# The three-valued weights of the second feed-forward layer, prepared one stage earlier

## The chip, the cores and the metric

The kernel runs on one core of one Trainium2 chip. The metric is the device time of one execution in microseconds; the median of three runs is shown. The core has five engines that run at the same time, each with its own queue of instructions that it works through in order: TensorE (PE, matrix products into PSUM; its weight loads are shown apart as PEld), VectorE (DVE), ScalarE (ACT), GpSimd (POOL), and SyncE (SP), which here only issues DMAs. They wait for each other by semaphores: an instruction raises one when it is done, and a wait in another engine's queue holds that queue until the count is reached. PSUM has eight banks of 128 x 512 fp32.

## The reference, cut to what matters

Eight layers run one after the other on x of 1024 rows and 512 columns, each as `x = x + layernorm(layer(layernorm(x)))`. The change touches the second feed-forward layer (L1 ffn), whose weight is made three-valued before it is used, and the attention ahead of it (L1 attention), in whose code it puts work:

```python
x = x + _layernorm(_L1_attn_ref(_layernorm(x), wq, bq, wk, bk, wv, bv))
x = x + _layernorm(_L1_ffn_ref(_layernorm(x), weight))     # weight: 512 out x 512 in

def _L1_ffn_ref(x, weight):
    def binarize_weights(weight):
        scale = mean(abs(weight), axis=1, keepdims=True)
        bin_no_grad = scale * sign(weight)
        clipped = clip(weight, -1.0, 1.0)
        return bin_no_grad - clipped + clipped
    return einsum('bsi,oi->bso', x, binarize_weights(weight))
```

The weights depend on no activation: they could be prepared at any time after their load.

## The kernel before, in words

The program is a row of blocks (`nc.Block()`). In a block every engine has its own code, and no engine begins the next block before all of them have come to the end of this one. Within a block the order of an engine's instructions is the order in which the code is written; there is no scheduler.

Around the change there are three blocks.

1. **The block of the L1 attention** (`small_attn`, name `l1a`, rope true). 32 heads in 8 groups of 4, each in 2 halves of the rows: 16 units of 16 steps, 256 steps in all (`TOTAL`). In a step PE makes two products of scores (L1654), ACT two exponentials of 128x512 (L1784), and PE the products of older exponentials with the values (L1671). DVE reduces the maxima of a later unit: one pair of tiles a step (`reduce_pair`, L1829), 24 steps ahead, so that the last pair stands at step 231. It also scales the finished output of a unit (`finish`, L1839 and L1842) when PE has turned it (`o_turn`, L1686): unit 14 at step 245, unit 15 behind the loop. In the last 16 steps PE adds a product of 128 columns per step that nobody reads (`idle`, L1679). The weight of L1 ffn is loaded by a DMA that SP issues after the first unit's maxima.
2. **The block of the norms** (`renorm`, class `Norms`). Two layer norms over eight tiles of 128 rows: DVE makes the statistics and the sum (L166 to L182), GpSimd the inverse root (L212), ACT the scaled tile `f` (L242), PE turns it with four transposes per tile into PSUM bank t (L282), and ACT copies it to `yT` (L260), the last but one by DVE. PE fills some of its waits with products that nobody reads (L271): six ahead of tile 4, five ahead of tile 6, three behind tile 7.
3. **The block of L1 ffn** (`l1_ffn`). DVE waits for the weight, takes the scale (L494, L496) and then, for each of four tiles `o` of 128 output rows, makes `pos` in six instructions of 128x512 (L500 to L510); a semaphore `s_b` counts them. PE turns each tile of `pos` with four transposes into banks 0 to 3 (L538), ACT copies it to `wT` (L519), and PE waits for all four copies (`pe.wait_ge(s_wT, KC)`). Then PE makes the rows: eight tiles of 128 rows, four products of 128x512 each (L544), 32 in all, which the trace shows as 64 since an fp32 product runs in two passes here. The norms of this layer follow in the same block, tile by tile behind the rows: DVE, GpSimd, ACT and PE by the same class `Norms`. SP's queue in this block issues the four loads of the next attention's weights (`l2a`).

Of the kernel before, what the change touches and what calls it, by code (L numbers as in the profile page):

```python
# [7 lines left out]
P = 128  # L8
T = 1024
NT = T // P  # L10
D = 512
KC = D // P
LN_EPS = 1e-5

ALU = mybir.AluOpType
ACT = mybir.ActivationFunctionType
AX = mybir.AxisListType
F32 = mybir.dt.float32
# [106 lines left out]
class Norms:  # L125
# [111 lines left out]
    def scale(self, act, n, p):  # L237

        chip, nc = self.chip, self.chip.nc
        act.wait_ge(chip.sem("ln_ready"), self.count("ready", (n, p), 1))  # L240
        for t in (2 * p, 2 * p + 1):
            nc.scalar.activation(chip.f[:, t, :], chip.x[:, t, :] if n else self.src(t), ACT.Identity,  # L242
                                 bias=chip.applied[:, n, 1, t:t + 1],
                                 scale=chip.applied[:, n, 0, t:t + 1]).then_inc(chip.sem("ln_scaled"), 1)
# [59 lines left out]
    return Norms(chip, True, chip.last, rows, src, turn_bank, by_halves)  # L304


def renorm(chip, add_f, loads=None):


    if chip.normed:  # L310
        chip.normed = False
        return
    norms = Norms(chip, bool(add_f), False, src=lambda t: chip.f[:, t, :], turn_bank=lambda t: t)
    with chip.nc.Block() as block:
        @block.sync
        def _(sp):
            if loads:
                loads(sp)

        @block.tensor  # L320
        def _(pe):
            norms.tensor(pe)

        @block.vector
        def _(dve):
            for k in range(len(norms.steps)):
                norms.vector(dve, k)
            norms.vector_end(dve)

        @block.gpsimd  # L330
        def _(pool):
            norms.gpsimd(pool)

        @block.scalar
        def _(act):
            norms.scalar(act)


# [120 lines left out]
def l1_ffn_weights(chip, a):  # L459

    w = Weights(chip, "l1f")
    w.w = w.sb("w", [P, KC, D])
    w.transfers(1)

    def loads(sp):
        w.load(sp, w.w[:], weights_view(a["l1f_w"]))
    w.loads = loads
    return w


def l1_ffn(chip, add_f):

    nc, ps, yT = chip.nc, chip.ps, chip.yT
    ahead = chip.take_ahead()
    w = ahead.w
    renorm(chip, add_f)
    s_row, b_row = chip.shared("rows", NT)
    s_b, s_t, s_wT = (chip.sem("l1f_" + n) for n in ("binary", "turned", "wT"))
    with ExitStack() as mem:
        def sb(n, shape, dt=F32):  # L480
            return mem.enter_context(nc.sbuf_tensor("l1f_" + n, shape, dt, side=ahead.side))
        pos, neg, wT = sb("pos", [P, KC, D]), sb("neg", [P, KC, D]), sb("wT", [P, KC, D])
        sc = sb("scale", [P, KC])

        def bank(t):
            return (4 + t) % 8
        following = chip.next_weights()
        norms = stage_norms(chip, (s_row, b_row), lambda t: ps[:, bank(t), :], bank)
        with nc.Block() as block:
            @block.vector  # L490
            def _(dve):
                ahead.wait(dve)
                n = 0
                nc.vector.tensor_reduce(sc[:], w[:], AX.X, ALU.add, apply_absolute_value=True).then_inc(s_b, 1)  # L494
                dve.wait_ge(s_b, 1)
                nc.vector.tensor_scalar(sc[:], sc[:], 1.0 / D, None, ALU.mult).then_inc(s_b, 1)  # L496
                dve.wait_ge(s_b, 2)
                for o in range(KC):
                    k = 2 + 6 * o
                    nc.vector.tensor_scalar(pos[:, o, :], w[:, o, :], 0.0, sc[:, o:o + 1], ALU.is_gt,  # L500
                                            ALU.mult).then_inc(s_b, 1)
                    nc.vector.tensor_scalar(neg[:, o, :], w[:, o, :], 0.0, sc[:, o:o + 1], ALU.is_lt,
                                            ALU.mult).then_inc(s_b, 1)
                    nc.vector.tensor_scalar(w[:, o, :], w[:, o, :], 1.0, -1.0, ALU.min, ALU.max).then_inc(s_b, 1)
                    dve.wait_ge(s_b, k + 3)
                    nc.vector.tensor_tensor(pos[:, o, :], pos[:, o, :], neg[:, o, :], ALU.subtract).then_inc(s_b, 1)
                    dve.wait_ge(s_b, k + 4)
                    nc.vector.tensor_tensor(pos[:, o, :], pos[:, o, :], w[:, o, :], ALU.subtract).then_inc(s_b, 1)
                    dve.wait_ge(s_b, k + 5)
                    nc.vector.tensor_tensor(pos[:, o, :], pos[:, o, :], w[:, o, :], ALU.add).then_inc(s_b, 1)  # L510
                for k in range(len(norms.steps)):
                    norms.vector(dve, k)
                norms.vector_end(dve)

            @block.scalar
            def _(act):
                for o in range(KC):
                    act.wait_ge(s_t, o + 1)
                    nc.scalar.copy(wT[:, :, o * P:(o + 1) * P],  # L519
                                   ps[:, o, :].rearrange("p (c q) -> p c q", c=KC)).then_inc(s_wT, 1)  # L520
                norms.scalar(act)

            @block.gpsimd
            def _(pool):
                norms.gpsimd(pool)

            @block.sync
            def _(sp):
                if following:
                    following.loads(sp)  # L530
                norms.sync(sp)

            @block.tensor
            def _(pe):
                for o in range(KC):
                    pe.wait_ge(s_b, 2 + 6 * (o + 1))
                    for c in range(KC):
                        mm = nc.tensor.transpose(ps[:, o, c * P:(c + 1) * P], pos[:, o, c * P:(c + 1) * P],  # L538
                                                 chip.ident[:])
                    mm.then_inc(s_t, 1)  # L540
                pe.wait_ge(s_wT, KC)
                for t in range(NT):
                    for c in range(KC):
                        mm = nc.tensor.matmul(ps[:, bank(t), :], yT[:, c, t * P:(t + 1) * P], wT[:, c, :],  # L544
                                              start=c == 0, stop=c == KC - 1)
                    mm.then_inc(s_row, 1)
                norms.tensor(pe)
    ahead.mem.close()
# [634 lines left out]
SPAN = T // HALVES  # L1183
# [92 lines left out]
def small_attn(chip, add_f, name, kv_heads, rope):  # L1276
# [3 lines left out]
    nc, ps, f, yT = chip.nc, chip.ps, chip.f, chip.yT  # L1280
# [5 lines left out]
    w = chip.take_ahead()  # L1286
# [3 lines left out]
    with ExitStack() as mem:  # L1290
        def sb(n, shape, dt=F32):
            return mem.enter_context(nc.sbuf_tensor(f"{name}_{n}", shape, dt, side=w.side))
# [3 lines left out]
        q = sb("q", [P, SLOTS, 2, T], F32R)  # L1296
        k = sb("k", [P, SLOTS, KP, T], F32R)
# [5 lines left out]
        mrow = sb("mrow", [4 * QT, P], F32R)  # L1303
        rden = sb("rden", [P, 2, QT, GROUP])
        if rope:
            tmp, res, ab = sb("tmp", [P, 4, SPAN]), sb("res", [P, 2, 2, SPAN]), sb("ab", [P, 2, 2, SPAN])
            s_bias, s_rot, s_pt, s_vb = (chip.sem(f"{name}_{n}") for n in ("biased", "rotated", "pool_rotated", "v_biased"))

        def by_heads(rows):
# [22 lines left out]
        TOTAL = UNITS * STEPS  # L1332
        BEFORE = PAIRS_OF_MAX + AHEAD
        BETWEEN = 18 if rope else BEFORE
        upto = [FIRST_PIECES + -(-(PIECES - FIRST_PIECES) * min(m, BETWEEN) // BETWEEN) for m in range(BEFORE + 1)]
        TAIL = TOTAL - STEPS
        FIRST_TURN = PAIRS_OF_MAX + 1

        s_proj, b_proj = chip.shared("sa_qk", NJ)
# [115 lines left out]
        with nc.Block() as block:  # L1455
# [338 lines left out]
            def _(dve):  # L1794
# [40 lines left out]
                def finish(n):  # L1835
                    g, half = divmod(n, HALVES)
                    dve.wait_ge(s_ot, b_ot + n + 1)
                    both = banks(("out", n))[:, 0, :].rearrange("p (t h e) -> p t h e", h=GROUP, e=2 * HD)
                    nc.vector.reciprocal(rden[:, n % 2], both[:, :, :, HD]).then_inc(s_rd, 1)  # L1839
                    dve.wait_ge(s_rd, b_rd + n + 1)  # L1840
                    rows = f[:, half * QT:(half + 1) * QT, g * GROUP * HD:(g + 1) * GROUP * HD]
                    nc.vector.tensor_tensor(rows.rearrange("p t (h e) -> p t h e", e=HD), both[:, :, :, 0:HD],  # L1842
                                            rden[:, n % 2].unsqueeze(3).broadcast_to([P, QT, GROUP, HD]),
                                            ALU.mult).then_inc(s_out, 1)
# [13 lines left out]
                for at in range(TOTAL):  # L1858
                    for m in max_at.get(at, []):
                        reduce_pair(m)  # L1860
                    n = unit_ended(at, TURN_OUT_STEP)
                    if n is not None:
                        finish(n)
                finish(UNITS - 1)
    if not rope:
        rows_out(chip, name, w)
# [974 lines left out]
```

## Time and profile before

| | |
|---|---|
| median of three runs | 2408.6 us (2408.6, 2408.64, 2401.95) |
| the profiled execution, its own time | 2398.62 us |
| its span in the trace | 2396.8 us |
| granted clock of PE, mean | 0.962 |
| PE busy | 2176.2 us (91%) |
| DVE busy | 1526.9 us (64%) |
| ACT busy | 1307.3 us (55%) |
| GpSimd busy | 643.5 us (27%) |
| the loop's last step to the first work of the norms | about 1413 to 1415.6 us in the trace |
| the block of the norms | 1415.6 to 1439.6 us |
| the block of L1 ffn | 1439.8 to 1499.7 us |

Times inside the trace are microseconds from the start of the span. The profiled execution is one execution, with the hardware profiler on. The busy shares are means over stages that are limited by different things; a change in one stage is read from that stage's rows alone. A row of the timeline gives the start, the duration from first to last instruction of the group, the engine, the line, what is written and read, and in brackets how long the engine had been idle and what ended that. The granted clock (PEclk) is the share of TensorE's full 2.4 GHz; 0.50 is 1.2 GHz.

### The profile page before, as it was taken

The numbers are of one execution on the slowest core, as the hardware profiler recorded it, in microseconds if no ns is written. First come the engines' busy times: TensorE is split into PE (matmuls) and PEld (weight loads), VectorE is DVE, ScalarE is ACT, GpSimd is POOL, SyncE is SP. The second block draws the span as 40 slices with busy tenths as digits, with TensorE's granted clock in tenths as the row PEclk, the third lists the DMA queues.
The fourth block names the chain that finished last, engine by engine and source line by source line (L and its number), as shares of the span: only waits on it lengthen the run. The fifth ranks groups of instructions, "written<-read, shape, count | busy, mean of one in ns | idle before, by whom it ended". The sixth has DMA issues, their size and how long they took to land. (4 is left out here: it accounts for less than half of the span.)

```text
span 2396.8 us, 35809 instructions
## 1 busy us (share of the span) xinstructions
PE 2176.2 (91%) x13122; PEld 1351.4 (56%) x13122; DVE 1526.9 (64%) x2211; ACT 1307.3 (55%) x2192; POOL 643.5 (27%) x529
## 2 busy tenths in 40 slices
PE   6998999999999798999999977799999998999877
PEld 4666777777777585444444444334444445877453
DVE  3575777777777434589999935149999935333253
ACT  4464777766767421238888862118888873312321
POOL 1574666666666301230000011200000003500110
PEclk9998999999999899999999988899999999999888
DMA  5681111111111321150011001530211104000010
GB/s 139 212 259 44 49 57 57 49 62 49 64 50 49 105 88 46 32 133 21 22 29 34 2 1 71 139 81 2 54 28 35 21 14 150 1 1 1 0 32 35
DMA packets 82924, 138.78 MB, mean 58 GB/s; under 512 B 31201, under 2 KB 41185, under 8 KB 82802
## 3 DMA queue, kind: packets, MB, share of 16 engines
q1 hardware_dynamic: 82802, 137.11, 19.5%
q8 instruction: 82, 1.34, 0.2%
q14 instruction: 40, 0.33, 0.0%
HBM read 95.65 MB, written 41.03 MB: 57 GB/s over the span
## 5 line engine op out<-in xcount | busy, mean ns | idle before, releaser
L2580 POOL TENSOR_TENSOR l0a_p_low<-yT,l0a_p_high 128x1024 fp32r<-128x1024 f32 (+7 forms) x256 | 389.2, 1539 | 237.7 <-ACT l0a_p_high L2604 236.3
L212 POOL TENSOR_TENSOR applied<-prepared,neghalf 128x2 f32<-128x2 f32 x64 | 50.1, 783 | 1261.4 <-DVE prepared L174 1261.4
L1829 DVE TENSOR_REDUCE l2a_mx<-ps 128x2 f32<-128x1024 f32 x256 | 310.4, 1224 | 48.6 <-PE ps L1635 47.6
L1829 DVE TENSOR_REDUCE l1a_mx<-ps 128x2 f32<-128x1024 f32 x256 | 310.3, 1225 | 34.2 <-PE ps L1635 33.0
L1784 ACT ACTIVATE l1a_prob<-ps 128x512 f32<-128x512 f32 x512 | 278.3, 596 | 67.6 <-PE ps L1654 49.3
L1784 ACT ACTIVATE l2a_prob<-ps 128x512 f32<-128x512 f32 x512 | 278.3, 596 | 62.7 <-PE ps L1654 43.7
L2642 DVE TENSOR_REDUCE l0a_mx<-ps 128x1 f32<-128x512 f32 (+3 forms) x384 | 206.5, 552 | 76.0 <-PE ps L2485 55.0
L2657 DVE TENSOR_TENSOR yT<-ps,l0a_mrows 128x1024 f32<-128x1024 f32 (+7 forms) x256 | 193.1, 754 | 88.6 <-PE ps L2509 80.9
L2598 ACT ACTIVATE yT<-yT 128x1024 f32<-128x1024 f32 (+7 forms) x256 | 175.2, 684 | 116.8 <-DVE yT L2657 116.8
L2604 ACT CAST l0a_p_high<-yT 128x1024 fp32r<-128x1024 f32 (+7 forms) x256 | 172.5, 674 | 14.3
L2485 PE MATMUL ps<-l0a_k_high,l0a_q_high 128*128 128x512 f32 (+3 forms) x384 | 143.0, 387 | 35.4 <-DVE l0a_mx L2642 23.8
L1671 PE MATMUL ps<-l1a_prob,l1a_vext 128*32 128x256 f32 x2048 | 159.6, 390 | 0.0
L1671 PE MATMUL ps<-l2a_prob,l2a_vext 128*32 128x256 f32 x2048 | 159.6, 390 | 0.0
L2507 PE MATMUL ps<-l0a_q_high,l0a_k_high 128*128 128x512 f32 (+3 forms) x384 | 138.7, 361 | 0.0
L2508 PE MATMUL ps<-l0a_q_low,l0a_k_high 128*128 128x512 f32 (+3 forms) x384 | 134.0, 349 | 0.0
L2519 PE MATMUL ps<-l0a_p_high,l0a_c_high 128*66 128x512 f32 (+3 forms) x384 | 128.5, 338 | 4.9 <-POOL l0a_p_low L2580 3.5
L2509 PE MATMUL ps<-l0a_q_high,l0a_k_low 128*128 128x512 f32 (+3 forms) x384 | 132.9, 346 | 0.0
L1635 PE MATMUL ps<-l2a_k,l2a_q 48*128 48x512 f32 x512 | 128.0, 497 | 3.0 <-DVE l2a_mx L1829 3.0
L1635 PE MATMUL ps<-l1a_k,l1a_q 48*128 48x512 f32 x512 | 128.0, 497 | 1.7 <-DMA l1a_q<-l1a_q_parts 1.6
L2519 PE MATMUL ps<-l0a_p_low,l0a_c_high 128*66 128x512 f32 (+3 forms) x384 | 129.5, 337 | 0.0
L2519 PE MATMUL ps<-l0a_p_high,l0a_c_low 128*66 128x512 f32 (+3 forms) x384 | 129.2, 337 | 0.0
L242 ACT ACTIVATE f<-x,applied 128x512 f32<-128x512 f32 x64 | 48.6, 808 | 131.7 <-POOL applied L217 131.5
(330 smaller groups left out, 4141.7 us busy)
## 6 DMA issues: line engine op xcount, KB each, us to landing
l0a_q<-l0a_q SPq DMA_DIRECT2D x32, 512.0 KB, 3.2
l0q_woh<-in_l0a_wo SPq DMA_DIRECT2D x16, 512.0 KB, 5.2
l0a_q<-f SPq DMA_DIRECT2D x32, 256.0 KB, 4.7
l0a_q<-l0q_q_pe SPq DMA_DIRECT2D x32, 256.0 KB, 3.6
l0a_recip_rows<-l0a_recip_row SPq DMA_DIRECT2D x32, 256.0 KB, 3.5
l0a_o<-l0a_o_pair SPq DMA_DIRECT2D x16, 512.0 KB, 2.8
yT<-l0a_o SPq DMA_DIRECT2D x16, 512.0 KB, 3.3
l2a_k<-l2a_k_parts SPq DMA_DIRECT2D x16, 256.0 KB, 4.3
```

Source lines behind the costliest of these rows:

```text
L1635: mm = nc.tensor.matmul(banks(("pair", m))[:, hf, :], q[rows, slot, p, qt * P:(qt + 1) * P], k[rows, slot, p % KP, 512 * c:512 * c + 512], ...
L1671: mm = nc.tensor.matmul(O[32 * hh:32 * hh + 32, cut], vext[:, j, g * GROUP + hh if OWN_KEYS else g, :], prob[:, j % 4, hh, cut], start=j = ...
L1784: nc.scalar.activation(prob[:, j % 4, 2 * p + hf, :], st(at, hf), ACT.Exp, scale=SCALE).then_inc(s_exp, 1)
L1829: nc.vector.tensor_reduce(mx[:, u % 2, :, p, t, c], banks(("pair", m)), AX.X, ALU.max).then_inc(s_red, 1)
L2485: mm = nc.tensor.matmul(b[:, 0:width], q_high[:, par, qt * P:(qt + 1) * P], k_high[:, 512 * c:512 * c + width], start=True, stop=dg is None)
L2507: nc.tensor.matmul(out, k_high[:, keys], q_high[:, par, lo:hi], start=True, stop=False)
L2519: mm = nc.tensor.matmul(OV[:, lo:hi], cc[:, j, :], pp[:, j % 4, lo:hi], start=j == 0 and k == 0, stop=k == 2 and j == (3 if hi == 512 else ...
L2580: nc.gpsimd.tensor_tensor(p_low[:, j % 4, P * j:T], prob[:, j % 4, P * j:T], p_high[:, j % 4, P * j:T], ALU.subtract).then_inc(s_pl, 1)
L2598: nc.scalar.activation(prob[:, j % 4, P * j:T], prob[:, j % 4, P * j:T], ACT.Exp, scale=SCALE).then_inc(s_exp, 1)
L2604: nc.scalar.copy(p_high[:, j % 4, P * j:T], prob[:, j % 4, P * j:T]).then_inc(s_ph, 1)
L2642: nc.vector.tensor_reduce(mx[:, qt, c:c + 1], bank(par, n)[:, 0:width], AX.X, ALU.max).then_inc(s_red, 1)
L2657: nc.vector.tensor_tensor(prob[:, j % 4, P * j:T], ST[j % 2][:, P * j:T], mrows[:, par, P * j:T], ALU.add).then_inc(s_less, 1)
```

## The change

DVE's instructions that make the weights three-valued leave the block of L1 ffn. They become two helpers, `scale` and `binarize`, of the weights' object, and the attention's DVE code calls them at five steps of its loop: the scale at step 236, and the four tiles at 238, 241, 246 and 249. PE's transposes of `pos` and ACT's copies to `wT` go to the head of their engines' code in the block of the norms, into banks 4 to 7 instead of 0 to 3, and so does PE's wait for the four copies. In the block of L1 ffn nothing of them is left. `pos` and the scale are allocated beside the loaded weight ahead of the attention, and the tile `neg` lies on the attention's `tmp`, which its loop does not use. The instructions are the same in number, shape and operands.

```diff
 def renorm(chip, add_f, loads=None, turn_weights=None, copy_weights=None):
         @block.tensor
         def _(pe):
+            if turn_weights:
+                turn_weights(pe)
             norms.tensor(pe)
         @block.scalar
         def _(act):
+            if copy_weights:
+                copy_weights(act)
             norms.scalar(act)
...
+    def scale(dve):
+        w.wait(dve)
+        nc.vector.tensor_reduce(sc[:], w.w[:], AX.X, ALU.add, apply_absolute_value=True).then_inc(s_b, 1)
+        dve.wait_ge(s_b, 1)
+        nc.vector.tensor_scalar(sc[:], sc[:], 1.0 / D, None, ALU.mult).then_inc(s_b, 1)
+        dve.wait_ge(s_b, 2)
+    def binarize(dve, o, neg):
+        k = 2 + 6 * o
+        nc.vector.tensor_scalar(pos[:, o, :], w.w[:, o, :], 0.0, sc[:, o:o + 1], ALU.is_gt, ALU.mult).then_inc(s_b, 1)
...
+        nc.vector.tensor_tensor(pos[:, o, :], pos[:, o, :], w.w[:, o, :], ALU.add).then_inc(s_b, 1)
...
+    def turn_weights(pe):
+        for o in range(KC):
+            pe.wait_ge(s_b, 2 + 6 * (o + 1))
+            for c in range(KC):
+                mm = nc.tensor.transpose(ps[:, 4 + o, c * P:(c + 1) * P], pos[:, o, c * P:(c + 1) * P], chip.ident[:])
+            mm.then_inc(s_t, 1)
+        pe.wait_ge(s_wT, KC)
+    def copy_weights(act):
+        for o in range(KC):
+            act.wait_ge(s_t, o + 1)
+            nc.scalar.copy(wT[:, :, o * P:(o + 1) * P],
+                           ps[:, 4 + o, :].rearrange("p (c q) -> p c q", c=KC)).then_inc(s_wT, 1)
+    renorm(chip, add_f, turn_weights=turn_weights, copy_weights=copy_weights)
...
             def _(dve):
-                ahead.wait(dve)
...
-                nc.vector.tensor_reduce(sc[:], w[:], AX.X, ALU.add, apply_absolute_value=True).then_inc(s_b, 1)
...
-                for o in range(KC):
...
             def _(pe):
-                for o in range(KC):
-                    pe.wait_ge(s_b, 2 + 6 * (o + 1))
...
-                    mm.then_inc(s_t, 1)
-                pe.wait_ge(s_wT, KC)
                 for t in range(NT):
...
+        TAIL_WORK = [TOTAL - 20, TOTAL - 18, TOTAL - 15, TOTAL - 10, TOTAL - 7]
...
                         finish(n)
+                    if rope and at in TAIL_WORK:
+                        k = TAIL_WORK.index(at)
+                        if k == 0:
+                            following.scale(dve)
+                        else:
+                            following.binarize(dve, k - 1, neg)
                 finish(UNITS - 1)
```

How the instructions stand on DVE from the end of the attention's maxima to the first norms. L1829 and L1832 (L1841 and L1844 in the changed kernel) are the reductions of the maxima, L1839 and L1842 (L1851 and L1854) are `finish` of units 14 and 15, and a branch ends a block. Before:

```order
L1829 TENSOR_REDUCE l1a_mx<-ps 128x2 x2
L1832 TENSOR_REDUCE l1a_mcol<-l1a_mx 128x16
L1839 RECIPROCAL l1a_rden<-ps 128x16
L1842 TENSOR_TENSOR f<-ps,l1a_rden 128x4x64
L1839 RECIPROCAL l1a_rden<-ps 128x16
L1842 TENSOR_TENSOR f<-ps,l1a_rden 128x4x64
L1455 UNCONDITIONAL_BRANCH
```

The changed kernel, on the same engine and in the same place, as far as the first of the four tiles (the second tile's six stand directly behind it, the third's and fourth's between the two `finish`):

```order
L1844 TENSOR_REDUCE l1a_mcol<-l1a_mx 128x16
L479 TENSOR_REDUCE l1f_scale<-l1f_w 128x4
L481 TENSOR_SCALAR l1f_scale<-l1f_scale 128x4
L487 TENSOR_SCALAR l1f_pos<-l1f_w,l1f_scale 128x512
L488 TENSOR_SCALAR l1f_neg<-l1f_w,l1f_scale 128x512
L489 TENSOR_SCALAR l1f_w<-l1f_w 128x512
L491 TENSOR_TENSOR l1f_pos<-l1f_pos,l1f_neg 128x512
L493 TENSOR_TENSOR l1f_pos<-l1f_pos,l1f_w 128x512
L495 TENSOR_TENSOR l1f_pos<-l1f_pos,l1f_w 128x512
```

The step numbers in the code fix only this order: between the last reduction and the `finish` of unit 14 there is nothing else in DVE's queue.

How PE stands from the end of the attention to the rows of L1 ffn. Before:

```order
L1686 MATMUL ps<-ident,l1a_osb 128x128 x4
L1455 UNCONDITIONAL_BRANCH
L320 UNCONDITIONAL_BRANCH
L282 MATMUL ps<-ident,f 128x128 x16
L271 MATMUL ps<-x,ident 128x256 x6
L282 MATMUL ps<-ident,f 128x128 x8
L271 MATMUL ps<-x,ident 128x256 x5
L282 MATMUL ps<-ident,f 128x128 x8
L271 MATMUL ps<-x,ident 128x256 x3
L314 UNCONDITIONAL_BRANCH
L533 UNCONDITIONAL_BRANCH
L538 MATMUL ps<-ident,l1f_pos 128x128 x16
```

The changed kernel, on PE over the same stretch:

```order
L1698 MATMUL ps<-ident,l1a_osb 128x128 x4
L1467 UNCONDITIONAL_BRANCH
L320 UNCONDITIONAL_BRANCH
L512 MATMUL ps<-ident,l1f_pos 128x128 x16
L282 MATMUL ps<-ident,f 128x128 x16
L271 MATMUL ps<-x,ident 128x256 x6
L282 MATMUL ps<-ident,f 128x128 x8
L271 MATMUL ps<-x,ident 128x256 x5
L282 MATMUL ps<-ident,f 128x128 x8
L271 MATMUL ps<-x,ident 128x256 x3
L314 UNCONDITIONAL_BRANCH
L549 UNCONDITIONAL_BRANCH
```

The sixteen transposes of the weights have gone from behind the norms to ahead of them, and the branch into the block of L1 ffn is now followed by the products of the rows. ACT's four copies to `wT` have made the same move.

## Rows read from the trace of the kernel before

**Rows 1.** Windows by stage: stretch, length, busy time of each engine, granted clock, DMA.
```profile
1340.00:1380.00 40.00, 38.32 (x365) 16.32 (x363) 36.62 (x35) 33.20 (x64) 0.00 (x0) 1.00 0.01 1
1380.00:1415.00 35.00, 32.69 (x305) 14.52 (x301) 1.04 (x4) 25.70 (x49) 0.00 (x0) 1.00 0.01 2
1515.00:1530.00 15.00, 15.00 (x36) 6.65 (x35) 1.79 (x3) 1.17 (x2) 0.00 (x0) 1.00 0.53 142
```

**Rows 2.** Timeline of the block of L1 ffn: start, duration, engine, line.
```profile
1439.89 2.29 DVE L494 TENSOR_REDUCE l1f_scale<-l1f_w 128x4 f32<-128x2048 f32 x1 [1.31 <-PEq L314]
...
1442.42 0.49 DVE L500 TENSOR_SCALAR l1f_pos<-l1f_w,l1f_scale 128x512 f32<-128x512 f32 x1
...
1445.73 0.48 DVE L500 TENSOR_SCALAR l1f_pos<-l1f_w,l1f_scale 128x512 f32<-128x512 f32 x1
...
1445.87 1.11 PE L538 MATMUL ps<-ident,l1f_pos 128*128 128x128 f32 x4 [6.28 <-DVE l1f_pos L510]
...
1456.94 0.59 ACT L519 COPY l1f_wT<-ps 128x512 f32<-128x512 f32 x1 [2.73 <-PE ps L538]
...
1457.58 30.21 PE L544 MATMUL ps<-l1f_wT,yT 128*128 128x512 f32 x64 [0.68 <-ACT l1f_wT L519]
```

**Rows 3.** Timeline: PE's end of the norms' block, and its start behind the next norms.
```profile
1438.13 1.46 PE L271 MATMUL ps<-x,ident 128*128 128x256 f32 x6
...
1500.02 6.25 PE L1591 MATMUL ps<-yT,l2a_wk 128*128 128x512 f32 x14 [0.30 <-PEq L489]
```

**Rows 4.** Windows of 2 us on PE: length, PE busy, granted clock, DMA.
```profile
1418.00:1420.00 2.00, 0.00 (x0) 0.56 0.00 0
...
1432.00:1434.00 2.00, 2.00 (x11) 1.00 0.00 0
...
1440.00:1442.00 2.00, 0.00 (x0) 1.00 0.29 88
1442.00:1444.00 2.00, 0.00 (x0) 0.53 0.97 345
...
1462.00:1464.00 2.00, 2.00 (x5) 0.85 0.00 0
```

**Rows 5.** Timeline: weight loads of L1 ffn's passes 3, 4, 8 and 64.
```profile
1458.60 0.34 PEld L544 LDWEIGHTS ps<-l1f_wT,yT 128*128 128x128 f32 x1 [0.52 <-issue]
1459.45 0.34 PEld L544 LDWEIGHTS ps<-l1f_wT,yT 128*128 128x128 f32 x1 [0.52 <-issue]
...
1462.74 0.19 PEld L544 LDWEIGHTS ps<-l1f_wT,yT 128*128 128x128 f32 x1 [0.39 <-issue]
...
1486.78 0.19 PEld L544 LDWEIGHTS ps<-l1f_wT,yT 128*128 128x128 f32 x1 [0.24 <-issue]
```

**Rows 6.** Timeline of DVE: the last two `finish`, with the idle time ahead of each.
```profile
1396.75 0.26 DVE L1839 RECIPROCAL l1a_rden<-ps 128x16 f32<-128x16 f32 x1 [17.18 <-PE ps L1686]
...
1414.60 0.26 DVE L1839 RECIPROCAL l1a_rden<-ps 128x16 f32<-128x16 f32 x1 [17.13 <-PE ps L1686]
```

**Rows 7.** Timeline, start and end of the norms' block on DVE, ACT and PE.
```profile
1415.64 1.29 DVE L166 BATCH_NORM_STATS2 stats<-f 128x6 f32<-128x512 f32 x2 [0.32 <-PEq L1455]
...
1423.24 1.52 ACT L242 ACTIVATE f<-x,applied 128x512 f32<-128x512 f32 x2 [9.38 <-POOL applied L217]
...
1424.10 1.97 PE L282 MATMUL ps<-ident,f 128*128 128x128 f32 x8 [9.54 <-ACT f L242]
...
1437.26 1.04 PE L282 MATMUL ps<-ident,f 128*128 128x128 f32 x8
```

**Rows 8.** SP's last issue of the next weights (start, its duration).
```profile
1441.39 0.91 SPq L356 DMA_DIRECT2D l2a_wo<-in_l2a_wo  x1
```

**Rows 9.** DMA issues from 1430 us: size, us from issue to landing.
```profile
l2a_wo<-in_l2a_wo SPq DMA_DIRECT2D x1, 1024.0 KB, 11.5
```

**Rows 10.** ACT's exponentials by form, from 1340 to 1380 and from 1380 to 1413 us.
```profile
L1784 ACT ACTIVATE l1a_prob<-ps 128x512 f32<-128x512 f32 x60 | 32.7, 596 | 6.8 <-PE ps L1654 4.5
...
L1784 ACT ACTIVATE l1a_prob<-ps 128x512 f32<-128x512 f32 x46 | 25.0, 595 | 6.0 <-PE ps L1654 5.2
```

More of the change, by code:

```diff
@@ L304, in stage_norms, with renorm @@
     return Norms(chip, True, chip.last, rows, src, turn_bank, by_halves)
-def renorm(chip, add_f, loads=None):
+def renorm(chip, add_f, loads=None, turn_weights=None, copy_weights=None):
     if chip.normed:
@@ L462, in l1_ffn_weights @@
     w.w = w.sb("w", [P, KC, D])
+    w.pos, w.sc = w.sb("pos", [P, KC, D]), w.sb("scale", [P, KC])
     w.transfers(1)
+    w.s_b = chip.sem("l1f_binary")
     def loads(sp):
@@ L467, in l1_ffn_weights @@
     w.loads = loads
+    nc, pos, sc, s_b = chip.nc, w.pos, w.sc, w.s_b
+    def scale(dve):
[7 more added lines that the diff above has]
+        nc.vector.tensor_scalar(pos[:, o, :], w.w[:, o, :], 0.0, sc[:, o:o + 1], ALU.is_gt, ALU.mult).then_inc(s_b, 1)
+        nc.vector.tensor_scalar(neg[:, o, :], w.w[:, o, :], 0.0, sc[:, o:o + 1], ALU.is_lt, ALU.mult).then_inc(s_b, 1)
+        nc.vector.tensor_scalar(w.w[:, o, :], w.w[:, o, :], 1.0, -1.0, ALU.min, ALU.max).then_inc(s_b, 1)
+        dve.wait_ge(s_b, k + 3)
+        nc.vector.tensor_tensor(pos[:, o, :], pos[:, o, :], neg[:, o, :], ALU.subtract).then_inc(s_b, 1)
+        dve.wait_ge(s_b, k + 4)
+        nc.vector.tensor_tensor(pos[:, o, :], pos[:, o, :], w.w[:, o, :], ALU.subtract).then_inc(s_b, 1)
+        dve.wait_ge(s_b, k + 5)
+        nc.vector.tensor_tensor(pos[:, o, :], pos[:, o, :], w.w[:, o, :], ALU.add).then_inc(s_b, 1)
+    w.scale, w.binarize = scale, binarize
     return w
@@ L474, in l1_ffn @@
     ahead = chip.take_ahead()
-    w = ahead.w
-    renorm(chip, add_f)
-    s_row, b_row = chip.shared("rows", NT)
[L478 to L483, printed above, removed]
+    pos = ahead.pos
+    wT = ahead.sb("wT", [P, KC, D])
+    s_b, s_t, s_wT = ahead.s_b, chip.sem("l1f_turned"), chip.sem("l1f_wT")
+    def turn_weights(pe):
[11 more added lines that the diff above has]
+    renorm(chip, add_f, turn_weights=turn_weights, copy_weights=copy_weights)
+    s_row, b_row = chip.shared("rows", NT)
+    if True:
         def bank(t):
@@ L491, in _ @@
             def _(dve):
-                ahead.wait(dve)
-                n = 0
-                nc.vector.tensor_reduce(sc[:], w[:], AX.X, ALU.add, apply_absolute_value=True).then_inc(s_b, 1)
-                dve.wait_ge(s_b, 1)
-                nc.vector.tensor_scalar(sc[:], sc[:], 1.0 / D, None, ALU.mult).then_inc(s_b, 1)
-                dve.wait_ge(s_b, 2)
-                for o in range(KC):
[L499 to L510, printed above, removed]
                 for k in range(len(norms.steps)):
@@ L516, in _ @@
             def _(act):
-                for o in range(KC):
-                    act.wait_ge(s_t, o + 1)
-                    nc.scalar.copy(wT[:, :, o * P:(o + 1) * P],
-                                   ps[:, o, :].rearrange("p (c q) -> p c q", c=KC)).then_inc(s_wT, 1)
                 norms.scalar(act)
@@ L534, in _ @@
             def _(pe):
-                for o in range(KC):
-                    pe.wait_ge(s_b, 2 + 6 * (o + 1))
-                    for c in range(KC):
-                        mm = nc.tensor.transpose(ps[:, o, c * P:(c + 1) * P], pos[:, o, c * P:(c + 1) * P],
-                                                 chip.ident[:])
-                    mm.then_inc(s_t, 1)
-                pe.wait_ge(s_wT, KC)
                 for t in range(NT):
@@ L1305, in small_attn @@
         if rope:
-            tmp, res, ab = sb("tmp", [P, 4, SPAN]), sb("res", [P, 2, 2, SPAN]), sb("ab", [P, 2, 2, SPAN])
+            tmp = chip.placed(mem, f"{name}_tmp", [P, 4, SPAN], F32, w.side)
+            res, ab = sb("res", [P, 2, 2, SPAN]), sb("ab", [P, 2, 2, SPAN])
+            neg = nc.alloc_sbuf_tensor_at("l1f_neg", [P, KC, D], F32, offset=chip.starts[f"{name}_tmp"])
             s_bias, s_rot, s_pt, s_vb = (chip.sem(f"{name}_{n}") for n in ("biased", "rotated", "pool_rotated", "v_biased"))
```

## The prediction, written before the changed kernel ran

> **What bounds the kernel now.** I began with the windows by stage. In the loop of the attention PE is the busy engine, but its last 35 us differ from the stretch before: DVE, busy 36.62 of 40 us while it reduces maxima, is busy 1.04 of 35 us behind them [rows 1]. Then I read the timeline of the block of L1 ffn. It opens with DVE alone: L494 starts at 1439.89, PE has its first tile to turn at 1445.87 after 6.28 us of idling, the last copy to `wT` starts at 1456.94, and only at 1457.58 does PE begin the products of the rows, which take 30.21 us [rows 2]. So two things stand in line there, 17.7 us of preparing weights and 30.2 us of products, and the rest of the block follows the last product. The 2 us windows show a third: PE's clock, 1.00 at 1432, is still 1.00 at 1440 to 1442 with PE idle, falls to 0.53 in the next window, and returns only with the products (0.85 at 1462) [rows 4]. The first products thus run at 1.2 GHz.
>
> **What is removed from the path.** The start: PE's last product that nobody reads ends at 1438.13 + 1.46 = 1439.59, and behind the same norms one layer later PE starts 0.30 us after the border [rows 3]. So the products can start at 1439.89, which is also where DVE starts now [rows 2]. They start at 1457.58 now: 17.69 us.
>
> The pace: passes 3 and 4 load 1459.45 - 1458.60 = 0.85 us apart; from pass 8 (1462.74) to pass 64 (1486.78) there are 56 steps in 24.04 us, 0.429 each [rows 5]. At 0.429 throughout, pass 64 would load 63 x 0.429 = 27.05 us after the start, where it now loads 1486.78 - 1457.58 = 29.20 us after it. That would be 2.15 us. But PE loads weights ahead of the pass, so the better measure is the whole group: 64 x 0.429 = 27.5 us, against 30.21: 2.7 us, in which the pipeline's last drain of some 0.15 us is not counted; I take 2.6. This holds if the clock is full at the start. The row that says so is 1440 to 1442, granted 1.00 [rows 4]: in the changed kernel dense products begin inside that window.
>
> Together 17.7 + 2.6 = 20.3 us earlier for the last product. Behind it DVE, GpSimd, ACT and PE do what they do now, paced by the rows, and the block after it follows.
>
> **What is added to the attention.** DVE's work is one scale, 1439.89 to 1442.42 = 2.53 us, and four tiles of 1445.73 - 1442.42 = 3.31 us [rows 2], 15.8 us in all. It moves into two holes: DVE idles 17.18 us before 1396.75 and 17.13 us before 1414.60, each time until PE has turned a unit [rows 6]. Into the first go the scale and two tiles, 2.53 + 6.62 = 9.15 us: from 1379.57 to 1388.7, 8.0 us before `finish` can start. Into the second go two tiles, 6.62 us from 1397.47 to 1404.1, 10.5 us early. The queue has nothing else behind them but the two `finish`, for which the block's end waits; the last maxima stand ahead of the scale, so the turn of the maxima and the scores do not wait. The wait for the loaded weight is met: SP issued that load after the first of 16 units. I cost this at nothing; if the cover were gone, the price would be what is over: 15.8 us at most.
>
> What the trace of before does not show is this work beside ACT's exponentials and PE's products. The nearest rows are the exponentials with DVE busy and with DVE idle, 596 and 595 ns [rows 10]: no effect, though DVE reads PSUM there and SBUF here. From below, a busier DVE can speed up nothing in this loop. From above, if each exponential over the 15.8 us took a tenth longer, 1.6 us. I take 0 and keep 1.6.
>
> **What is added to the norms.** Sixteen transposes at the head of PE's queue, four copies at the head of ACT's. `pos` has long been ready. PE can start where DVE does, near 1415.6 [rows 7]. At full clock eight transposes take 1.04 us [rows 7], so sixteen 2.1 us; at half clock four take 1.11 us [rows 2], so 4.4 us. ACT starts a copy 1.1 us after a tile's first transpose and needs 0.59 [rows 2]: done at about 1415.6 + 3 x 0.59 + 1.1 + 0.6 = 1419.1, or at half clock 1415.6 + 3 x 1.11 + 1.1 + 0.6 = 1420.6. Behind these stand ACT's first scaling, which waits for GpSimd until 1423.24, and PE's first turn at 1424.10 [rows 7]. So 2.6 us are spare at the least, and PE's new wait for the four copies holds nobody. DVE's chain of statistics, which sets this block's length, is not touched. Cost 0; from above, 1.5 us if both started late by 4 us; no gain, since nothing that DVE or GpSimd waits for here comes from PE or ACT.
>
> **What is moved past what.** SP's queue keeps its four loads for the next attention at the head of the block of L1 ffn. They now run beside the products rather than ahead of them. The last is issued from 1441.39 on, in 0.91 us, and lands 11.5 us after its issue [rows 8, 9], about 1453 to 1454. It is wanted where the next block starts, now 1500.0 and then 1479.7: 26 us early. Do the products suffer beside 345 GB/s? The nearest row has 142 GB/s from 1515 to 1530, with PE busy throughout and 36 passes in 15 us (0.417 each) at full clock [rows 1]. From above, if the passes beside the 14 us of loads ran a tenth slower, 1.4 us. I take 0.
>
> **Clock, row and rule.** The clock fell to 0.56 in the window 1418 to 1420 after PE had ended the attention's last turns at 1414.6 [rows 6], and was 1.00 at 1432 after PE had worked on the norms from 1424.10 [rows 4, 7]. The change puts 2 to 4 us of transposes into the front of that gap, and I expect the fall a little later and the same return. The products' first 5 us decide 2.6 us.
> The Trainium skill, "TensorE: Matmul & The Clock Gate", Part 1 on the clock gate, says that the half rate is the default and activity releases it, and that the same kernel showed 6, 11 or 14 cold matmuls from run to run, as the gate's timing is not tied to the program. By that rule the return at 1432 is luck in part, and a run could reach 1439.9 still at half clock. The trace shows one execution and cannot exclude it; it is the first rival.
>
> **The sum.** 17.7 + 2.6 - 0 = 20.3 us. Against the profiled execution, 2398.62 (its span 2396.8 and 1.8 around it), that is 2378.3. The runs shown lie higher, 2401.95 to 2408.64 with a median of 2408.6, which would give 2388.3; the middle of all four executions, 2405.3, gives 2385.0. I forecast 2387, in between and nearer to the median shown.
>
> **Rivals.**
> 1. *The products start at half clock* (chance 0.13). For it: the norms' PE work is thin and the gate was low until about 1432. Against it: 8 us at 1.00 behind that. Then the 2.6 us stay, the gain is 17.7 us, and if the norms' last turns are slow too (1.04 us becomes 2.1, and the last products that nobody reads 1.46 become 2.6) some 2 us less: 15.5 to 17.7, thus 2391 to 2393.
> 2. *Part is given back in the attention's tail, beside the loads or in the norms* (0.10): the upper ends above, 1.6 + 1.5 + 1.4 = 4.5 us; gain 15.8, thus 2393.
> 3. *The change does not do what it says* (0.03): DVE reaches the tiles late, because the attention's end waits for `finish` of unit 15 behind them. It needs the second hole's 6.62 us to become more than 17.1, 2.6 times as long. All 15.8 us of work would then show in front of the norms, and 4.5 us of the gain remain (2.6 and what PE and ACT hide, 1.9): 2404.
> 4. *Slower* (0.03): the added turns at the head of the norms upset the return of the clock, and PE does the whole of L1 ffn at 1.2 GHz. 64 passes of 0.853 are 54.6 us from 1439.9, so the last product ends at 1494.5 instead of 1487.8: 6.7 us later, and half-speed turns in the norms behind it (16 and 14 others) add 2 to 4: +9 to +11 us, 2418. It is slower than now from the 48th cold pass on, (17.7 + 30.2 - 27.5) / 0.424. Against it: in dense products the clock came back within 5 us of 1457.58 [rows 2, 4].
>
> **How the numbers follow.** The forecast has 0.71, with its own spread of 2379 to 2391 from the runs' level and the small bounds. A measurement of this kernel can tell about 0.3%, 7.2 us, from no change; the forecast and the first two rivals lie beyond it, though the level of the runs moves by as much as that, so I leave 0.05 of their 0.94 to "no difference". Faster 0.89, within 0.3% 0.08, slower 0.03. The range is 2377 (the profiled execution's level less 20.3, and one more) to 2397 (the median less 12).
>
> **What would show it.** In the changed profile: DVE's L479 starts directly behind L1844, and the two `finish` start where they do now, with about 8 and 10.5 us of idling ahead of them. PE's transposes of `l1f_pos` stand near 1415.6, the first `f` L242 at 1423.2, PE's block of norms ends at 1439.6. L553 starts at 1439.9, lasts 27.6 us, and the clock is 1.00 throughout it. The next attention's first product is at 1479.7. Wrong would be: a later `finish`, steps of the tail longer than now, an L553 of 30 us, or a wait on the l2a loads.

## The result, and the profile after

The changed kernel is faster: 2378.6 us (median of nine runs, 2376.27 to 2388.48) against 2402.25 (nine runs, 2392.89 to 2408.64). The ratio is 0.9911 with a 95% interval of 0.9899 to 0.9924, so the gain is 18 to 24 us, 21.4 in the middle. The two medians lie 23.65 us apart. The forecast gain was 20.3 us. The stated time of 2387 was 8.4 us too high. It is 2407.3 less 20.3, and the median of before is now 2402.25: 5.05 of the 8.4 us are the level it was counted from.

The profiled execution took 2377.18 us, with a span of 2375.4, 21.4 less than before. Two executions differ elsewhere too, so the reading goes by a piece that holds all of the change and little else: from the start of the attention's last reduction of maxima (`l1a_mcol`) to the start of the next attention's first product. Before it is 1379.39 to 1500.02, **120.63 us**; here 1378.20 to 1478.62, **100.42**: 20.21 less. I call it the stage below. (The 1500.02 is in [rows 3]. The 1379.39 is this row of the kernel before, whose end [rows 6] put at 1396.75 - 17.18 = 1379.57.)

```profile
1379.39 0.19 DVE L1832 TENSOR_REDUCE l1a_mcol<-l1a_mx 128x16 f32<-128x32 f32 x1
```

DVE's timeline behind the maxima, in the changed kernel:

```profile
1378.20 0.18 DVE L1844 TENSOR_REDUCE l1a_mcol<-l1a_mx 128x16 f32<-128x32 f32 x1
1378.31 2.27 DVE L479 TENSOR_REDUCE l1f_scale<-l1f_w 128x4 f32<-128x2048 f32 x1
...
1386.83 0.69 DVE L495 TENSOR_TENSOR l1f_pos<-l1f_pos,l1f_w 128x512 f32<-128x512 f32 x1
1395.57 0.26 DVE L1851 RECIPROCAL l1a_rden<-ps 128x16 f32<-128x16 f32 x1 [8.05 <-PE ps L1698]
...
1402.20 0.69 DVE L495 TENSOR_TENSOR l1f_pos<-l1f_pos,l1f_w 128x512 f32<-128x512 f32 x1
1413.42 0.26 DVE L1851 RECIPROCAL l1a_rden<-ps 128x16 f32<-128x16 f32 x1 [10.52 <-PE ps L1698]
...
1414.45 1.29 DVE L166 BATCH_NORM_STATS2 stats<-f 128x6 f32<-128x512 f32 x2 [0.32 <-PEq L1467]
```

The two holes of 17.18 and 17.13 us [rows 6] have shrunk to 8.05 and 10.52, and that is all: from the start of L1844 to the last `finish` it is 35.22 us, against 35.21 from L1832 before. The instructions take as long as in their old place (the scale's reduction 2.27 us against 2.29). The exponentials beside them do too:

```profile
L1796 ACT ACTIVATE l1a_prob<-ps 128x512 f32<-128x512 f32 x44 | 23.9, 596 | 5.9 <-PE ps L1666 5.2
```

596 ns, as in [rows 10]. PE's and ACT's timeline through the norms into L1 ffn and out of it:

```profile
1414.45 1.94 PE L512 MATMUL ps<-ident,l1f_pos 128*128 128x128 f32 x16 [1.07 <-PEq L1467]
...
1423.00 1.94 PE L282 MATMUL ps<-ident,f 128*128 128x128 f32 x8 [6.61 <-ACT f L242]
...
1429.35 3.55 PE L271 MATMUL ps<-x,ident 128*128 128x256 f32 x12
...
1436.93 1.46 PE L271 MATMUL ps<-x,ident 128*128 128x256 f32 x6
1438.69 27.70 PE L553 MATMUL ps<-l1f_wT,yT 128*128 128x512 f32 x64 [0.30 <-PEq L314]
...
1478.62 7.10 PE L1603 MATMUL ps<-yT,l2a_wk 128*128 128x512 f32 x16 [0.30 <-PEq L528]
```
```profile
1415.12 2.05 ACT L519 COPY l1f_wT<-ps 128x512 f32<-128x512 f32 x4 [2.45 <-PE ps L512]
1422.04 1.52 ACT L242 ACTIVATE f<-x,applied 128x512 f32<-128x512 f32 x2 [4.87 <-POOL applied L217]
```

The sixteen transposes and four copies are over at 1417.2, and ACT then idles 4.87 us for GpSimd as it idled 9.38 before [rows 7]. The block of the norms takes 24.24 us from its first statistics (1414.45) to the products (1438.69); before, from 1415.64 to 1439.89, it was 24.25 [rows 2, 7]. The products begin 0.30 us behind the border and take 27.70 us instead of 30.21. The windows on PE, 2 us long (length, PE busy, granted clock, DMA share, GB/s):

```profile
1418.00:1420.00 2.00, 0.00 (x0) 1.00 0.00 0
1420.00:1422.00 2.00, 0.00 (x0) 0.68 0.00 0
...
1430.00:1432.00 2.00, 2.00 (x8) 0.76 0.00 0
1432.00:1434.00 2.00, 1.95 (x14) 1.00 0.00 0
...
1440.00:1442.00 2.00, 2.00 (x6) 1.00 0.77 266
1442.00:1444.00 2.00, 2.00 (x6) 1.00 1.01 336
...
1448.00:1450.00 2.00, 2.00 (x6) 1.00 1.05 408
```

One of these windows in the kernel before:

```profile
1430.00:1432.00 2.00, 2.00 (x8) 0.53 0.00 0
```

The clock falls a window later than in [rows 4], returns within the same window (0.76 against 0.53, and 1.00 in the next), and is full under the products. The loads of the next attention's weights run beside the first half of them, at up to 408 GB/s.

### The profile page after: what moved, and what is told of

The parts are those of the page before. It is cut to its first block and busy times, and to the rows that moved or that the text cites. A ratio compares the mean times of both kernels' runs of the same rounds, so it can differ in the third digit from the quotient of the medians.

```text
span 2375.4 us, 35810 instructions
## 1 busy us (share of the span) xinstructions
PE 2167.8 (91%) x13122; PEld 1346.8 (57%) x13122; DVE 1528.4 (64%) x2211; ACT 1306.9 (55%) x2192; POOL 641.9 (27%) x529
## 5 line engine op out<-in xcount | busy, mean ns | idle before, releaser
L1841 DVE TENSOR_REDUCE l2a_mx<-ps 128x2 f32<-128x1024 f32 x256 | 310.4, 1224 | 48.6 <-PE ps L1647 47.6
L1841 DVE TENSOR_REDUCE l1a_mx<-ps 128x2 f32<-128x1024 f32 x256 | 310.2, 1224 | 32.9 <-PE ps L1647 31.6
L1666 PE MATMUL ps<-l2a_q,l2a_k 49*128 49x512 f32 x512 | 108.1, 419 | 11.8 <-ACT l2a_prob L1796 10.3
```

The costliest lines, as they stand in the source:

```text
L1841: nc.vector.tensor_reduce(mx[:, u % 2, :, p, t, c], banks(("pair", m)), AX.X, ALU.max).then_inc(s_red, 1)
```

## The experiments

Each profile gives the stage of one execution; the ratio is to the kernel before on the same chip. "Changed" is the changed kernel. Fillers are products that nobody reads, put in to keep PE busy.

| | stage, from and to | stage, us | ratio (95%) |
|---|---|---|---|
| before | 1379.39 to 1500.02 | 120.63 |  |
| changed | 1378.20 to 1478.62 | 100.42 | 0.9911 (0.9899 to 0.9924) |
| changed, again (e8) | 1379.32 to 1479.74 | 100.42 | 0.9915 (0.9902 to 0.9929) |
| e1 turns stay in L1 ffn | 1376.92 to 1480.15 | 103.23 | 0.9934 (0.9913 to 0.9955) |
| e2 DVE's work in the norms | 1376.97 to 1493.60 | 116.63 | 0.9979 (0.9970 to 0.9989) |
| e3 before, PE kept busy | 1380.38 to 1498.54 | 118.16 | 1.0002 (0.9989 to 1.0014) |
| e4 first hole overrun | 1383.07 to 1483.76 | 100.69 | one execution |
| e5 second hole overrun | 1379.93 to 1484.41 | 104.48 | one execution |
| e6 no fillers in the norms | 1385.58 to 1488.06 | 102.48 | 0.9912 (0.9895 to 0.9928) |
| e7 norms and L1 ffn merged | 1381.45 to 1471.95 | 90.50 | 0.9869 (0.9853 to 0.9884) |
| e9 merged, PE kept busy | 1386.81 to 1477.33 | 90.52 | 0.9866 (0.9844 to 0.9889) |

**e1: DVE's part alone.**

```diff
-    renorm(chip, add_f, turn_weights=turn_weights, copy_weights=copy_weights)
+    renorm(chip, add_f)
...
             def _(act):
+                copy_weights(act)
                 norms.scalar(act)
...
             def _(pe):
+                turn_weights(pe)
                 for t in range(NT):
```

> DVE's work is in the attention as in the changed kernel, but the sixteen transposes and four copies stay at the head of the block of L1 ffn. Measured by the stage from the last reduction of maxima (start) to the next attention's first product: 120.63 us before, 100.42 changed. Theory: with all four tiles ready, the turns and copies overlap, first copy 0.8 us after the border, then 4 x 0.59: the products start 3.2 us later than in the changed kernel, still at full clock, stage 103.6. So DVE's move alone is worth 17 of the 20.2 us. Rival: turn and copy go one after the other for each tile as before (4 x 1.75): 7 us later, 107.4, and a cold start of the products on top (2.5).

```profile
1437.42 1.94 PE L512 MATMUL ps<-ident,l1f_pos 128*128 128x128 f32 x16 [0.30 <-PEq L314]
1440.19 27.73 PE L555 MATMUL ps<-l1f_wT,yT 128*128 128x512 f32 x64 [0.83 <-ACT l1f_wT L519]
```

103.23 us. The products start 2.77 us behind the turns' start, and at full clock. So the move of DVE's work, with the clock that comes with it, is worth 17.4 of the 20.2 us, and the move of the turns 2.8. I had put 103.6; the rival would have needed 107.4.

**e2: the same work at the head of the norms' block.**

```diff
         def _(dve):
+            if make_weights:
+                make_weights(dve)
             for k in range(len(norms.steps)):
                 norms.vector(dve, k)
...
-                    if rope and at in TAIL_WORK:
+                    if False:
```

> DVE's work stands at the head of its code in the block of the norms instead of in the attention's loop; turns and copies as in the changed kernel. Theory: the norms' block is set by DVE's chain of statistics, so the 15.8 us show in full: stage 100.4 + 15.8 = 116.2; what is left of the gain is the clock and the turns, some 4 us against before. Rival: GpSimd, ACT and PE set the norms' block in part, and some of the work hides: under 110.

```profile
1413.24 2.29 DVE L481 TENSOR_REDUCE l1f_scale<-l1f_w 128x4 f32<-128x2048 f32 x1 [0.33 <-PEq L1475]
...
1429.01 1.28 DVE L166 BATCH_NORM_STATS2 stats<-f 128x6 f32<-128x512 f32 x2
```
```profile
1443.90 4.27 PE L271 MATMUL ps<-x,ident 128*128 128x256 f32 x12
1448.01 1.04 PE L282 MATMUL ps<-ident,f 128*128 128x128 f32 x8
...
1453.68 27.70 PE L561 MATMUL ps<-l1f_wT,yT 128*128 128x512 f32 x64 [0.30 <-PEq L314]
```

116.63 us, 16.2 more than changed. DVE's work stands in front of the first statistics for 1429.01 - 1413.24 = 15.77 us, and all of it shows, since DVE sets the length of that block. The remaining 0.4 are fillers that ran longer at half clock: from the start of those ahead of tile 4 to the next turns it takes 4.11 us instead of 3.39, and 0.28 come back in these turns. It is not "earlier" that pays but "where DVE has nothing else".

**e3: the clock alone.**

```diff
                 for o in range(KC):
+                    for _ in range(12 if o == 0 else 5):
+                        nc.tensor.matmul(ps[:, 7, 0:256], chip.ident[:], chip.x[:, 0, 0:256], start=True, stop=True)
                     pe.wait_ge(s_b, 2 + 6 * (o + 1))
```

> The kernel before, with products that nobody reads put in front of each of PE's four waits for a tile of weights (12, 5, 5, 5 of 256 columns, into bank 7). Theory: the first five us of L1 ffn's products were slow by the clock alone; with it kept up the group L544 takes 27.7 us instead of 30.2, stage 120.6 - 2.5 = 118.1. Rival: they were slow from something else (the copies just made, the loads beside them), or the fillers delay the turns: 30.2 us, stage 120.6 or more.

```profile
1457.26 0.66 PE L540 MATMUL ps<-ident,l1f_pos 128*128 128x128 f32 x4 [0.49 <-DVE l1f_pos L510]
1458.59 27.73 PE L546 MATMUL ps<-l1f_wT,yT 128*128 128x512 f32 x64 [0.68 <-ACT l1f_wT L519]
```

The products take 27.73 us instead of 30.21, and the turn of four takes 0.66 instead of 1.11 [rows 2]: the slow start was the clock. In the whole time it does not show: the ratio is 1.0002, and its interval begins at 0.9989, just where a gain of 2.5 us would lie (0.9990). The trace of one execution shows the gain in the stage; the whole times do not show one, and why is open.

**e4 and e5: how much room the two holes have.** The edit is e4's; in e5 the condition is `k == 4` and the count 20.

```diff
                             following.binarize(dve, k - 1, neg)
+                        if k == 2:
+                            s_fill = chip.sem("filled")
+                            dve.wait_ge(following.s_b, 2 + 6 * k)
+                            for i in range(16):
+                                nc.vector.tensor_tensor(neg[:, k - 1, :], neg[:, k - 1, :], neg[:, k - 1, :],
+                                                        ALU.max).then_inc(s_fill, 1)
+                                dve.wait_ge(s_fill, i + 1)
```

> The changed kernel with sixteen more DVE instructions (maximum of a tile of neg with itself, 0.727 us each, 11.6 us) behind the second tile of weights, ahead of the scaling of unit 14, where 8.05 us are spare. Theory: that scaling starts 3.6 us late, nobody waits for it but the next DVE work, whose 10.5 us of room take it: stage 100.4. Rival: a late scaling holds PE or the block's end: 104.0.

> The changed kernel with twenty more such DVE instructions (14.5 us) behind the fourth tile, ahead of the scaling of unit 15, where 10.52 us are spare. Theory: the scaling is 4.0 us late and the block ends with it: stage 104.4, with the exponentials and products beside them as long as before. Rival: DVE's load on SBUF is what costs, not its lateness: the steps of the tail get longer and the stage grows by more than 4.0; or nothing waits for the scaling, 100.4.

Their `finish` of units 14 and 15, first in e4, then in e5 (the last maxima begin at 1383.07 and 1379.93):

```profile
1404.05 0.26 DVE L1851 RECIPROCAL l1a_rden<-ps 128x16 f32<-128x16 f32 x1
...
1418.31 0.26 DVE L1851 RECIPROCAL l1a_rden<-ps 128x16 f32<-128x16 f32 x1 [6.94 <-PE ps L1698]
```
```profile
1397.31 0.26 DVE L1851 RECIPROCAL l1a_rden<-ps 128x16 f32<-128x16 f32 x1 [8.06 <-PE ps L1698]
...
1419.20 0.26 DVE L1851 RECIPROCAL l1a_rden<-ps 128x16 f32<-128x16 f32 x1
```

In e4 the first `finish` starts 20.98 us behind the maxima instead of 17.37, without a wait, and the second on time: the stage stays, but for 0.27 us of slower fillers. In e5 the last `finish` is 39.27 us behind the maxima instead of 35.22, and the stage grows by 4.06, the 4.05 that it is late. DVE, busy without a break beside ACT and PE, made nothing else longer: the exponentials take 596 ns in both. So the order in the queue decides, and the room behind the second pair of tiles, 10.5 us, is the one that counts.

**e6: without the fillers of these norms.**

```diff
-            for _ in range(n):
+            for _ in range(n if fill else 0):
...
-            norms.tensor(pe)
+            norms.tensor(pe, fill=not turn_weights)
```

> The changed kernel without the fourteen products that nobody reads in the block of the norms ahead of L1 ffn. Theory: PE is then too thin there, the clock is still at half when the products begin: 2.5 us more in them, about 1 us more in the last turns, 0.65 us less at the border, where PE's fillers end last: stage 103.3. Rival: the clock comes back by the turns alone, and only the 0.65 us shows: 99.8.

```profile
1443.52 1.97 PE L282 MATMUL ps<-ident,f 128*128 128x128 f32 x8 [1.39 <-ACT f L242]
1446.42 29.42 PE L553 MATMUL ps<-l1f_wT,yT 128*128 128x512 f32 x64 [0.93 <-PEq L314]
```
```profile
1446.00:1448.00 2.00, 1.58 (x2) 0.50 0.38 18
1448.00:1450.00 2.00, 2.00 (x4) 0.53 0.84 301
1450.00:1452.00 2.00, 2.00 (x6) 1.00 0.95 331
```

This is the first rival's cold start, made to happen by leaving the fillers out: the products start at half clock and take 29.42 us, 1.7 more; the last turns take 1.97 instead of 1.04, which the time saved at the border does not quite pay. 102.48 us, 2.06 more than changed; I had put 2.9, with 2.5 us of it in the products: the clock was full again from about 1450 on, so the cold start cost less than in the kernel before. The profiled execution (2388.48 us) was some 10 us longer than the other three; it had reached the stage 7.4 us later than changed, so most of that lies ahead of the stage. Whether the products start at half clock in the other three is not shown. The ratios of e6 and changed (0.9912 and 0.9911) do not tell them apart.

**e7: what the early weights make possible.** With the weights ready ahead of the norms, a tile's rows need only that tile of `yT`. The two blocks become one, and PE works off this list; the norms turn into banks 4 to 7, the rows lie in banks 0 to 7.

```diff
+PE_ORDER = [("turn", 0), ("turn", 1), ("row", 0), ("turn", 2), ("turn", 3), ("row", 1), ("turn", 4), ("turn", 5),
+            ("row", 2), ("turn", 6), ("turn", 7)] + [("row", t) for t in range(3, NT)]
...
+                def row(t):
+                    first.wait_tile(pe, "copied", t if t < 4 else NT - 1)
```

> The changed kernel with the block of the norms and the block of L1 ffn made one: since the weights are ready before the norms, PE makes the rows of a tile between the turns of later tiles (rows 0, 1 and 2 between the four pairs of turns, 3 to 7 behind), the fillers of these norms are left out, the norms turn into banks 4 to 7 and the rows lie in banks 0 to 7. Theory: PE, idle 12 of 25 us in the norms, is then bound by its own work from the first turn on: 6 further turned tiles 3.1 us and 27.5 us of products, 3 us more for the half clock at the start: last product some 34 us after the first turn, instead of 43.4: stage 92 to 94, time 7 us or 0.3% less than the changed kernel. Rival: the products, slow at half clock, delay the turns of later tiles, and with them ACT and the norms' chain, and take back half or more of it: 97 or worse.

> The changed kernel again, beside the merged one on the same chip: stage 100.4 and a ratio to the kernel before of 0.991.

```profile
1426.25 1.94 PE L566 MATMUL ps<-ident,f 128*128 128x128 f32 x8 [6.62 <-ACT f L242]
1428.02 5.05 PE L573 MATMUL ps<-l1f_wT,yT 128*128 128x512 f32 x8
1432.90 1.04 PE L566 MATMUL ps<-ident,f 128*128 128x128 f32 x8
1433.78 3.60 PE L573 MATMUL ps<-l1f_wT,yT 128*128 128x512 f32 x8
1437.21 1.04 PE L566 MATMUL ps<-ident,f 128*128 128x128 f32 x8
...
1442.39 17.33 PE L573 MATMUL ps<-l1f_wT,yT 128*128 128x512 f32 x40
...
1471.95 7.10 PE L1627 MATMUL ps<-yT,l2a_wk 128*128 128x512 f32 x16 [0.30 <-PEq L532]
```

90.50 us, 9.9 less than changed, and 2367.9 us against 2378.0 for the changed kernel on the same chip (0.9869 against 0.9915; the intervals do not touch). I had put 92 to 94: the 34 us of my own sum against 43.4 would have given 91.0, and the range added a margin that was not needed. PE works without a gap from 1426.25 to the last product at 1459.7, 33.5 us. The later tiles' turns do come late (1432.90 where changed would have 1430.8), but the norms' chain of statistics on DVE runs through without a wait and is over at 1436.5; only DVE's copy of the last but one tile waits for them (5.66 us), ahead of the rows' statistics, and PE has rows to work on meanwhile. This version beats both kernels.

**e9: the same, with PE kept busy ahead of the norms.**

```diff
                 turn_weights(pe)
+                for _ in range(11):
+                    nc.tensor.matmul(ps[:, 3, 0:256], chip.ident[:], wT[:, 0, 0:256], start=True, stop=True)
```

> The merged kernel with eleven products of 256 columns that nobody reads (into bank 3) between the wait for the weights' copies and the first turn of the norms, where PE idled 6.62 us and its clock fell to 0.50. Theory: the clock stays at full, the first eight turns take 1.04 us instead of 1.94 and row 0's products 3.60 instead of 5.05; some of it is lost where PE then waits for ACT's scaled tiles: stage 89.0 against 90.5. Rival: in the merged block the pace of the first half is ACT's and GpSimd's chain, not PE's: 90.2 or more.

```profile
1423.06 2.96 PE L516 MATMUL ps<-ident,l1f_pos 128*128 128x128 f32 x16 [1.08 <-PEq L1493]
1426.70 6.94 PE L579 MATMUL ps<-l1f_wT,ident 128*128 128x256 f32 x22 [0.68 <-ACT l1f_wT L523]
1433.47 1.04 PE L566 MATMUL ps<-ident,f 128*128 128x128 f32 x8
```

90.52 us: no gain, and inconclusive for both theories. In this execution the clock had fallen during the weights' turns already (2.96 us instead of 1.94), the fillers ran at half speed for the most part, took 6.94 us instead of some 4.9 (ten passes take 2.32 us in the norms, six 1.46), and held the first turn 1.9 us longer than its tile needed; what the warm start then saved went into that. Whether fewer of them would pay is open.

## Why the prediction was right

The mechanism and each term of the sum held, in the stage; the two gains measure 17.70 + 2.51 = 20.21 us, which is all of the difference:

- *The start of the products.* Forecast 17.69 us earlier; by the norms' first statistics as the mark, they start 24.24 us behind it instead of 1457.58 - 1415.64 = 41.94 [rows 2, 7]: 17.70. e1 and e2 split it and show its condition.
- *The pace of the products.* Forecast 2.6 us; measured 30.21 - 27.70 = 2.51. e3 shows that it is the clock, and e6, in one profile, that it depends on PE's fillers in the norms: without them 1.72 of it are lost.
- *DVE in the attention at nothing*, with 8.0 and 10.5 us left over: 8.05 and 10.52, and 35.22 us against 35.21. e4 and e5 make it more than an absence of change: past 10.5 us the cost comes, one for one. The third rival named a real wait, as e5 shows, but its condition was not met; e2 shows its price, all 15.8 us in front of the norms, where 4.0 us of the gain are left in the stage and I had put 4.5. With the exponentials at 596 ns, the first of the three parts of the second rival (1.6 us kept for contention) is refuted too.
- *Turns and copies in the norms at nothing.* The block takes 24.24 us against 24.25. The copies end at 1417.2, 2.7 us into the block; I had put 3.5 at full clock (1419.1 - 1415.6): the first copy starts 0.67 us behind the first turn, where I took the 1.1 us that [rows 2] show at half clock, and the four copies take 2.05 us instead of 4 x 0.59. That the turns ran at full clock is luck: in e4 and e6 the same turns took 3.16 and 2.98 us, still without holding the first scaled tile.
- *The loads beside the products at nothing.* With loads of up to 408 GB/s beside their first half the 64 passes take 27.70 us, against 27.73 in e3, whose products have no loads beside them. The nearest row was misread: the 36 passes in 15 us count those cut by the window's edges. The timeline of before has (1527.56 - 1520.69) / 16 = 0.429 us a pass there, the same pace as elsewhere, so the conclusion stands.
- *The last three products that nobody reads* end the norms' block, as before.

Where it was off is the absolute time, and the step that was off is the choice of the level: I counted 2387 from 2407.3, near the median shown, and the median of before was itself 6 us lower in nine runs than in three. The other 3.35 us are that the medians lie 23.65 apart and not 20.3. That the sum made against the profiled execution, 2378.3, comes so near to 2378.6 is luck: that execution lay 3.6 us below the median of before, and the 3.35 us cancel this. The stage's 20.2 lies inside the interval of the gain by the ratio, 18 to 24 with 21.4 in the middle.

The fourth rival, products at 1.2 GHz throughout, was not seen in any profile. In the seven profiles of kernels with these fillers and two separate blocks (changed, e8 and e1 to e5) the products took 27.70 to 27.73 us, so the first rival was not seen in them either. They are one execution each.

## What to carry to other kernels

Work that depends on no activation belongs where its engine waits for others, and the trace says how much fits: the idle time ahead of each instruction that stays, and whether anybody waits for that instruction. The same 15.8 us cost nothing in the attention's tail and 16.2 us at the head of a block that DVE itself bounds. Once such work is out of the way, ask what its absence allows: here the border between two blocks had lost its reason, and removing it, with PE's rows put between the turns, gave half as much again as the change.

## What the runs showed that I had not expected

- The same sixteen transposes of the weights, in the same place behind the attention and behind the same 1.07 or 1.08 us of idling, took 1.94 us in changed, e7 and e8, and 2.96, 2.98 and 3.16 in e9, e6 and e4: the clock fell under them in some executions and not in others. (In e5 they took 3.50, but there PE had idled 5.11 us and the clock was at 0.50 already.) Likewise the twelve passes of fillers ahead of tile 4 took 3.41 to 4.30 us. Neither moved the stage by more than 0.5 us, but it makes a filler a gamble, as e9 shows. The Trainium skill, "TensorE: Matmul & The Clock Gate", Part 1, says that the number of cold matmuls changes from run to run because the gate runs free of the program; these rows agree, as far as kernels with the same code up to there can show it.
- Much of the spread of whole executions lies ahead of the stage. Changed and e8 have it at 100.42 both. Yet it began between 1376.92 (e1) and 1386.81 us (e9), although the code ahead of it is the same: executions differ by up to 10 us before they reach it. On one chip, e1 and e6 stand together at 65.1 us, in the first layer; e6 is 4.3 us behind at the end of the same group of products (172.6 and 176.9), 5.4 at 1002.8 and 1008.2, and 8.7 at the stage. Why is open. A difference of 2 us, as in e3 and e6, can be read in a piece of the trace and not in medians of ten or of four runs.
